# Attention outputs split on GpSimd and turned by DMA, with the K projection, its store and its stack at earlier steps

## The chip, the cores and the metric

One core of a Trainium2 chip runs the whole kernel. The metric is the device time of one execution in microseconds (us). Engines are named as in the profile: PE is TensorE's matmul, PEld its weight load, DVE is VectorE, ACT is ScalarE, POOL is GpSimd, and SP is SyncE, whose queue issues nearly all DMAs here.

## What is computed

A gated cross-attention block and a gated mixture of experts, for 16 sequences of 512 tokens, 256 wide:

```python
x = x + tanh(g_xattn) * (attention(layernorm(x), ctx) @ Wo.T + bo)    # 16 heads of 16, causal, softmax
x = x + tanh(g_ffn) * experts(layernorm(x))                           # 8 experts, each takes the top 128 tokens of a sequence
```

The mask is causal over the context too, so only the first 512 of its 1601 rows count. Float32 results come out of bf16 matmuls by splitting a number into a high part (its bf16 rounding) and a low part (what is left, in bf16), and summing three products for each 128 rows of the contraction.

## The kernel before

The program has two phases. `attention` takes the first 890 us or so, `experts` the rest; the change touches the first alone.

**Bodies and steps.** `steps(b)` (lines 77 to 122) writes the order of the attention phase out by hand. A body b has 4 groups of heads, g = 0 to 3, and 11 steps in each, k = 0 to 10. Below, *step 2.3* is g = 2, k = 3. In step g.k stands first the unit `max` of (b, g, k): matmuls of Q by K into one of three PSUM banks in turn, whose row maximum DVE takes (4 reductions over whole units of small tiles, 8 custom instructions for the 384 and 512 wide tiles); so PE can be three units ahead of DVE and no more. Behind it stands `sc` for k up to 9, the scores of the group two earlier, whose exponential ACT takes and whose diagonal blocks POOL zeroes (`affine_select`, behind `sc` 7, 8 and 9). Then come the pieces of the table `extra`. Every engine walks the same list and does its own part of each piece, in that order, so that a piece that waits holds up all pieces behind it on its engine. `rounds` (line 290) runs the bodies -1 to 17: -1 fills, 16 and 17 drain, 3 to 13 are a loop. One body works for several sequences: `max` for b, the projections for b + 1, the end of the attention for b - 1, and output, second layernorm and router for b - 2.

**The pieces that the texts speak of.**
- `ln1`, `ln1+`: statistics and application of the first layernorm (DVE, lines 628 to 641; a power on POOL, line 773). `xsplit`, `csplit`: POOL splits the layernorm's output and the context into high and low parts, a bf16 cast (line 792) and a subtraction (line 794) for each half. `xturn`, `cturn`: SP issues two DMA transposes (line 348).
- `q`, `k`, `v`: projections (PE, lines 510 and 523). `q+`, `k+` take the results to three bf16 parts (ACT line 604, DVE line 685, POOL lines 778 and 780). `qstore`, `kstore` write them to DRAM (SP, line 340), `qstack`, `kstack` load them stacked by group (SP, line 360).
- `mt`, `mt+`, `mrow`: the row maxima are turned by PE (line 485), split (ACT line 588, DVE line 671), and written by two small DMAs (line 370) into the rows that `sc` of that group contracts with. `mt` of (b, g) stands a group behind its maxima.
- `pv`, `pv+`: probabilities by V into one bank (PE line 477), copied by ACT. `yt`: PE turns the result back (line 490). `yt+`: DVE divides by the sum into `yq` (lines 693 and 697).
- `yb`: PE turns half of `yq`, 128 columns, with four float32 transposes (line 500). `yb+`: ACT takes the high part (line 599), DVE the low part (line 677), into `ynT`. `o`: PE multiplies by Wo (line 523). `o+`: DVE adds to the residual (line 709).

**Banks.** All of `yt`, `yb`, `mt`, `o`, `q`, `k`, `xt`, `ll`, `lt` and `v` are jobs. They use two PSUM banks in turn, in the order of the list, and `free_bank` makes each wait until the job two places before it has been read.

Of the kernel before, what the change touches and what calls it, by code (L numbers as in the profile page):

```python
# [79 lines left out]
def steps(body):  # L80
# [1147 lines left out]
```

## Time and profile before

| | |
|---|---|
| median of 3 runs | 1950.83 us (1948.68 to 1951.47) |
| the profiled execution | 1948.92 us |
| its span, first to last instruction | 1947.0 us |
| mean granted TensorE clock | 0.981 |
| PE, PEld busy | 1795.8 us (92%), 1063.0 us (55%) |
| DVE, ACT, POOL busy | 1133.9 us (58%), 893.9 us (46%), 868.6 us (45%) |
| DMA queue of SP | 204.13 MB, 44.9% of 16 engines' span |

Busy shares are averages over both phases. In the timeline of an engine a row may stand for several equal instructions (x4); a bracket at its end gives how long the engine was idle before it and what released it. The end of a matmul is modelled, about 0.16 us later than the next one's start, so on PE the time of a piece is read from start to start.

### The profile page before, as it was taken

Reading aid. Unit: us, or ns where it says so; the run is one execution under the profiler, and the core shown is the slowest. Engines: PE = TensorE matmul, PEld = TensorE weight load, DVE = VectorE, ACT = ScalarE, POOL = GpSimd, SP = SyncE. Lnnn points to the kernel's source line nnn. Section 1 sums busy time; section 2 is a strip of 40 time slices with the busy share of each in tenths; the row PEclk is TensorE's granted clock in tenths of the full one; section 3 lists DMA queues with packets and bytes.
Section 4 is the critical chain, followed back from the end, with each engine's and each line's share of the span. In section 5 each row is a group of like instructions: output and inputs, shape, how many; then the busy total and the mean of one; then the engine's idle time right before and its main releaser. Section 6 shows DMA issues by size and latency. Waiting matters only on the chain.

```text
span 1947.0 us, 41394 instructions
## 1 busy us (share of the span) xinstructions
PE 1795.8 (92%) x13478; PEld 1063.0 (55%) x13542; DVE 1133.9 (58%) x2809; ACT 893.9 (46%) x1716; POOL 868.6 (45%) x899
## 2 busy tenths in 40 slices
PE   3899999999999999981899999999999999999997
PEld 1455555555555555551365665656555656656565
DVE  2778888888888888756744344343424343443431
ACT  1366666656556666652334334343434343343332
POOL 4466666666666666445042423233233324232322
PEclk9899999999999999995999999999999999999999
DMA  6767666666666666527554564645546646445222
GB/s 150 167 153 166 161 161 171 166 164 161 169 162 155 170 160 165 136 68 183 141 109 89 101 118 86 120 95 90 106 75 121 123 87 103 83 81 96 49 31 25
DMA packets 377497, 239.30 MB, mean 123 GB/s; under 512 B 259479, under 2 KB 358943, under 8 KB 377375
## 3 DMA queue, kind: packets, MB, share of 16 engines
q1 hardware_dynamic: 352799, 204.13, 44.9%
q0 software_dynamic: 24576, 33.57, 11.0%
q8 instruction: 73, 1.20, 0.3%
q14 instruction: 49, 0.40, 0.1%
HBM read 118.63 MB, written 58.72 MB: 91 GB/s over the span
## 4 chain that ended last, share of the span: by engine, by line
PE 49%; DVE 2%; SPq 1%; DMA 1%; issue 1%; ACT 0%; POOL 0%; POOLq 0%; DVEq 0%
PE bank L1085 11%; PE bank L1084 11%; PE bank L1086 10%; PE bank L1102 6%; PE bank L1100 6%; PE bank L1101 6%; SPq L1011 1%; DVE h L1202 0%; DVE h L1205 0%; ACT h L1130 0%; DMA gate_raw<-in_L_ffn_w_gate 0%; DVE top_at L1152 0%; DVE work L1155 0%; POOL gate_nat L1029 0%; SPq L990 0%
## 5 line engine op out<-in xcount | busy, mean ns | idle before, releaser
L1050 POOL DMA_INDIRECT out<-y,row_now x128 | 202.0, 1578 | 604.4 <-ACT y L1137 579.7
L574 ACT ACTIVATE prob<-bank 128x512 f32<-128x512 f32 x640 | 368.8, 598 | 173.5 <-PE bank L463 88.1
L1202 DVE TENSOR_TENSOR h<-bank,silu 128x512 f32<-128x512 f32 x256 | 176.3, 689 | 396.7 <-PE bank L1086 262.0
L1130 ACT ACTIVATE h<-h 128x512 bf16<-128x512 f32 x256 | 161.2, 630 | 346.9 <-DVE h L1202 331.5
L661 DVE CUSTOM_DVE_ANT_0 masked<-bank,causal 128x384 f32<-128x384 f32 (+1 forms) x512 | 299.0, 616 | 35.8 <-PE bank L440 34.5
L440 PE MATMUL bank<-ks,qs 96*128 96x128 bf16 (+3 forms) x1024 | 278.3, 306 | 20.7 <-DMA ks<-k_parts 10.4
L1205 DVE TENSOR_TENSOR h<-h 128x512 bf16<-128x512 f32 x256 | 177.3, 693 | 179.6 <-ACT h L1130 173.3
L1101 PE MATMUL bank<-downT,h 128*128 128x256 bf16 x1024 | 279.1, 273 | 0.0
L1102 PE MATMUL bank<-downT,h 128*128 128x256 bf16 x1024 | 279.1, 273 | 0.0
L1100 PE MATMUL bank<-downT,h 128*128 128x256 bf16 x1024 | 279.1, 273 | 0.0
L1085 PE MATMUL bank<-tokT,gateT 128*128 128x512 bf16 x511 | 194.4, 380 | 35.4 <-DMA tokT<-rows 30.2
L813 POOL TENSOR_SCALAR_AFFINE_SELECT prob<-prob 128x512 f32<-128x512 f32 x256 | 159.2, 646 | 110.5 <-ACT prob L574 110.4
L460 PE MATMUL bank<-qs,ks 128*128 128x128 bf16 x1024 | 198.6, 220 | 3.2 <-ACT prob L574 0.9
L1084 PE MATMUL bank<-tokT,upT 128*128 128x512 bf16 x511 | 194.4, 380 | 6.8 <-DVE h L1202 6.7
L463 PE MATMUL bank<-qs,ks 98*128 98x384 bf16 (+2 forms) x768 | 196.3, 273 | 0.0
L1085 PE MATMUL bank<-tokT,upT 128*128 128x512 bf16 x512 | 194.6, 380 | 0.1
L1086 PE MATMUL bank<-tokT,upT 128*128 128x512 bf16 x512 | 194.6, 380 | 0.0
L477 PE MATMUL bank<-prob,v_aug 128*32 128x512 f32 (+3 forms) x2048 | 190.5, 444 | 1.4 <-ACT yT L582 1.4
L1084 PE MATMUL bank<-tokT,gateT 128*128 128x512 bf16 x481 | 182.8, 380 | 2.5 <-ACT silu L1124 0.9
L440 PEld LDWEIGHTS bank<-ks,qs 96*128 96x128 bf16 x1024 | 99.3, 98 | 154.7 <-issue 60.9
L1086 PE MATMUL bank<-tokT,gateT 128*128 128x512 bf16 x481 | 182.9, 380 | 0.1
L1137 ACT ACTIVATE y<-bank,gate_now 128x256 f32<-128x256 f32 x128 | 53.7, 470 | 260.8 <-PE bank L1102 260.8
(146 smaller groups left out, 2931.0 us busy)
## 6 DMA issues: line engine op xcount, KB each, us to landing
q_parts<-q_sb SPq DMA_DIRECT2D x64, 192.0 KB, 2.9
k_parts<-k_sb SPq DMA_DIRECT2D x64, 192.0 KB, 2.9
qs<-q_parts SPq DMA_DIRECT2D x64, 192.0 KB, 2.9
ks<-k_parts SPq DMA_DIRECT2D x64, 192.0 KB, 3.3
x_t<-in_x SPq DMA_DIRECT2D x16, 512.0 KB, 3.9
ctx_t<-in_ctx SPq DMA_DIRECT2D x16, 512.0 KB, 4.8
qs<-q_parts SPq DMA_DIRECT2D x64, 128.0 KB, 2.9
ks<-k_parts SPq DMA_DIRECT2D x64, 128.0 KB, 3.2
```

The source lines that it names most:

```text
L440: last = nc.tensor.matmul(dst[:, h * w:(h + 1) * w], qs[0:STACK, gr, h0 + h, i * P:(i + 1) * P], ks[0:STACK, gr, h0 + h, 0:w], start=True, ...
L460: last = nc.tensor.matmul(dst[:, at:at + P], ks[:, gr, h0 + h, j * P:(j + 1) * P], qs[:, gr, h0 + h, j * P:(j + 1) * P], start=True, stop= ...
L463: last = nc.tensor.matmul(dst[:, at + P:at + PWIDTH[j]], ks[0:ROWS, gr, h0 + h, j * P:(j + 1) * P], qs[0:ROWS, gr, h0 + h, (j + 1) * P:T], ...
L574: nc.scalar.activation(prob[:, gr % 2, h0:h0 + nh, POFF[tiles[0]]:POFF[tiles[0]] + w], sc_bank[SC_BANK[k]][:, 0:nh * w].rearrange("p (h w) ...
L661: nc.vector.tensor_tensor_reduce(masked[:, k % 2, 0:w], max_bank[max_at(gr, k)][:, 0:w], causal[:, T - w:T], 1.0, LOWEST, ALU.add, ALU.max ...
L1050: nc.gpsimd.indirect_dma_start(out_rows, bass.IndirectOffsetOnAxis(ap=row_now[:, par, c, s:s + 1], axis=0), y[:, c % 2, s, :], None, compu ...
L1084: nc.tensor.matmul(banks[it % 2][:, :], hi, xh, start=(dh == 0), stop=False)
L1085: nc.tensor.matmul(banks[it % 2][:, :], hi, xl, start=False, stop=False)
L1086: last = nc.tensor.matmul(banks[it % 2][:, :], lo, xh, start=False, stop=(dh == NH2 - 1))
L1100: nc.tensor.matmul(to, hh, wh, start=(it == 0), stop=False)
L1101: nc.tensor.matmul(to, hh, wl, start=False, stop=False)
L1102: last = nc.tensor.matmul(to, hl, wh, start=False, stop=(it == IT - 1))
```

## The change

- `yb` and `yb+` go. In their place stand `ysplit` on POOL (a cast and a subtraction on half of `yq`, into `y_nat`) and `yturn` on SP (one DMA transpose of that half, both parts, into `ynT`, which has another layout). `o` waits for the transposes, and `yt+` waits for `ysplit` where it waited for `yb`.
- Half 0 is split at step 1.3 and turned at step 1.6, half 1 at 3.3 and 3.9, where `yturn` stands behind the stacks.
- `ln1+` goes from steps 0.0 and 0.1 to 0.2 and 0.4, `xsplit` from 0.1 and 0.2 to 0.3 and 0.5, `xturn` from 0.5 to 0.7.
- The K projection goes from steps 2.4 and 2.5 to 2.1 and 2.4, `kstore` from 3.0 to 2.9, `kstack` of group 0 from 3.6 to 3.3.
- `mt` of group 1 goes from step 2.1 to 2.2, its `mrow` from 2.2 to 2.3. `pv` of group 3 goes from steps 2.1, 2.2, 2.4, 2.5 to 2.3, 2.5, 2.6, 2.7, its `pv+` from 2.7 to 2.9, `yt` and `yt+` of group 2 from 2.3 and 2.2 to 2.7 and 2.6, `qstack` of group 0 from 3.3 to 3.1.
- `masked`, the output of DVE's custom instruction that nothing reads, becomes bf16.

```diff
     extra = {
-        0: {0: [("pv", b - 1, 1, 0), ("ln1+", b + 1, 0)],
-            1: [("yt", b - 1, 0), ("pv", b - 1, 1, 1), ("xsplit", b + 1, 0), ("ln1+", b + 1, 1)],
-            2: [("yt+", b - 1, 0), ("yb", b - 2, 1), ("xsplit", b + 1, 1)],
+        0: {0: [("pv", b - 1, 1, 0)],
+            1: [("yt", b - 1, 0), ("pv", b - 1, 1, 1)],
+            2: [("yt+", b - 1, 0), ("ln1+", b + 1, 0)],
...
-            3: [("yt", b - 1, 2), ("yb", b - 1, 0), ("yb+", b - 1, 0), ("k+", b + 1, 0)],
...
-    masked = sb(ctx, "masked", [P, 2, T], F32)
+    masked = sb(ctx, "masked", [P, 2, T], BF16)
...
+                elif kind == "yturn":
+                    half = p[2]
+                    hold(split_lo["y"], count(b, 2, half + 1))
+
+                    hold(filled["o"], count(b, 2, 0))
+                    sp.dma_start_transpose(ynT[:, half, :, :, :].rearrange("p r i t -> p (r i) t"),
+                                           y_nat[:, half, :, :, :].rearrange("p r i d -> p (r i d)"))\
+                        .then_inc(flipped["y"], 16)
...
-                            wait(pe, read["yb"], count(b, 2, 2))
+                            wait(pe, flipped["y"], count(b, 32, 32))
...
-                elif kind == "yb+":
-
-                    half = p[2]
-                    wait(dve, hi_done[job], count(b, 2, half + 1))
-                    nc.vector.tensor_tensor(ynT[:, 1, half, :], src[:, :], ynT[:, 0, half, :], ALU.subtract)\
-                        .then_inc(read[job], 1)
...
-                    wait(dve, filled["yb"], count(b, 2, gr // 2 - 1))
+                    wait(dve, split_lo["y"], count(b, 2, gr // 2 - 1))
...
+                elif kind == "ysplit":
+                    half = p[2]
+                    wait(pool, read["yt"], count(b, GROUPS, 2 * half + 2))
+
+                    wait_apart(pool, flipped["y"], count(b, 32, 16 * half - 16), passed["pool"])
+                    src = yq[:, :, half * P:(half + 1) * P]
+                    nc.gpsimd.tensor_copy(y_nat[:, half, 0, :, :], src).then_inc(split_hi["y"], 1)
+                    wait(pool, split_hi["y"], count(b, 2, half + 1))
+                    nc.gpsimd.tensor_tensor(out=y_nat[:, half, 1, :, :], in0=src, in1=y_nat[:, half, 0, :, :],
+                                            op=ALU.subtract).then_inc(split_lo["y"], 1)
```

The places where the order of instructions moves most are shown as rows of each engine's program, in the body behind the loop (b = 14), which has the loop's order. `ISA` is the custom maximum, and the lines of the changed kernel are a few higher or lower than before.

DVE at the start of group 0, before (`mx` are the maxima of steps 0.0 to 0.3):

```order
L666 TENSOR_REDUCE mx<-bank 128x4
L641 TENSOR_SCALAR xn<-x_t,ln_mv,ln_rstd 128x256 x2
L666 TENSOR_REDUCE mx<-bank 128x2
L641 TENSOR_SCALAR xn<-x_t,ln_mv,ln_rstd 128x256 x2
L666 TENSOR_REDUCE mx<-bank 128x2
L693 RECIPROCAL rden<-bank 128x16
L697 TENSOR_TENSOR yq<-bank,rden 128x4x64
L661 ISA masked,mx<-bank,causal 128x384
L661 ISA mx 128x1
L677 TENSOR_TENSOR ynT<-bank,ynT 128x512
```

and now:

```order
L667 TENSOR_REDUCE mx<-bank 128x4
L667 TENSOR_REDUCE mx<-bank 128x2 x2
L688 RECIPROCAL rden<-bank 128x16
L692 TENSOR_TENSOR yq<-bank,rden 128x4x64
L642 TENSOR_SCALAR xn<-x_t,ln_mv,ln_rstd 128x256 x2
L662 ISA masked,mx<-bank,causal 128x384
L662 ISA mx 128x1
```

The division into `yq` now stands ahead of both halves of the layernorm, and the second half of the layernorm two steps further down.

PE at steps 2.1 and 2.2, before, from the end of the scores of step 2.1:

```order
L460 MATMUL bank<-qs,ks 128x128
L463 MATMUL bank<-qs,ks 128x256
L460 MATMUL bank<-qs,ks 128x128
L485 MATMUL bank<-ident,mx 16x128
L477 MATMUL bank<-prob,v_aug 32x512 x4
L440 MATMUL bank<-ks,qs 128x256
L444 MATMUL bank<-mask_qk,identb 128x128
L440 MATMUL bank<-ks,qs 128x256
L444 MATMUL bank<-mask_qk,identb 128x128
L460 MATMUL bank<-qs,ks 128x128
L463 MATMUL bank<-qs,ks 128x384
L477 MATMUL bank<-prob,v_aug 32x384 x4
```

and now:

```order
L469 MATMUL bank<-qs,ks 128x128
L472 MATMUL bank<-qs,ks 128x256
L469 MATMUL bank<-qs,ks 128x128
L515 MATMUL bank<-cT,wkT 128x512 x6
L449 MATMUL bank<-ks,qs 128x256
L453 MATMUL bank<-mask_qk,identb 128x128
L449 MATMUL bank<-ks,qs 128x256
L453 MATMUL bank<-mask_qk,identb 128x128
L469 MATMUL bank<-qs,ks 128x128
L472 MATMUL bank<-qs,ks 128x384
L494 MATMUL bank<-ident,mx 16x128
L449 MATMUL bank<-ks,qs 128x384
```

Six matmuls of K, and the maximum of step 2.2, now stand between the start of group 2 and the turn of the maxima of group 1, and the `pv` matmuls stand behind it.

SP at the end of group 0 and in group 1, now (before, the row with `ynT` was not there):

```order
L349 DMA_TRANSPOSE cT<-c_nat 128x8x128 x2
L146 ISA
L356 DMA_TRANSPOSE ynT<-y_nat 128x8x128
L146 ISA
L146 REGISTER_ALU
L379 DMA qs<-m_sb 1x16x128 x2
```

The transpose of `yq`'s first half stands between the context's transposes and the rows of the maxima of group 0.

## Rows read from the trace of the kernel before

**Rows 1.** Groups 0 to 3 of a body: us, busy PE, PEld, DVE, ACT, POOL, clock, DMA.

```profile
495.94:509.73 13.79, 12.42 (x123) 8.09 (x124) 12.10 (x35) 7.39 (x14) 9.57 (x12) 1.00 0.58 157
509.73:520.96 11.23, 11.01 (x99) 5.54 (x99) 10.24 (x34) 7.23 (x15) 5.40 (x8) 1.00 0.64 136
520.96:535.13 14.17, 13.26 (x115) 7.07 (x115) 11.24 (x30) 8.25 (x17) 9.71 (x11) 1.00 0.81 223
535.13:547.12 11.99, 11.85 (x131) 7.83 (x132) 9.34 (x32) 8.03 (x18) 7.69 (x10) 1.00 0.53 132
```

**Rows 2.** Timeline of PE, body at 496 to 547 us: groups 0 to 2.

```profile
500.13 0.60 PE L500 MATMUL bank<-ident,yq 128*128 128x128 f32 x4
500.56 0.33 PE L440 MATMUL bank<-ks,qs 96*128 96x384 bf16 x1
...
503.50 0.27 PE L485 MATMUL bank<-ident,mx 128*16 128x128 f32 x1 [1.31 <-DVE yq L697]
...
513.51 1.46 PE L510 MATMUL bank<-xT,wqT 128*128 128x512 bf16 x6
...
520.90 0.23 PE L440 MATMUL bank<-ks,qs 96*128 96x128 bf16 x1 [0.22 <-DVE mx L661]
...
523.10 0.28 PE L485 MATMUL bank<-ident,mx 128*16 128x128 f32 x1 [0.79 <-DVE mx L661]
...
525.76 0.34 PE L440 MATMUL bank<-ks,qs 96*128 96x384 bf16 x1
...
527.58 1.47 PE L510 MATMUL bank<-cT,wkT 128*128 128x512 bf16 x6
```

**Rows 3.** Timeline of DVE in the same body, groups 0 to 2.

```profile
499.06 0.74 DVE L641 TENSOR_SCALAR xn<-x_t,ln_mv,ln_rstd 128x256 f32<-128x256 f32 x2
...
500.31 1.74 DVE L641 TENSOR_SCALAR xn<-x_t,ln_mv,ln_rstd 128x256 f32<-128x256 f32 x2
...
503.76 0.69 DVE L677 TENSOR_TENSOR ynT<-bank,ynT 128x512 bf16<-128x512 f32 x1
...
506.29 0.75 DVE L709 SCALAR_TENSOR_TENSOR x<-bank,tanh_g,res_t 128x512 f32<-128x512 f32 x1 [0.71 <-PE bank L523]
...
510.74 1.88 DVE L666 TENSOR_REDUCE mx<-bank 128x4 f32<-128x512 f32 x3
...
524.23 1.27 DVE L666 TENSOR_REDUCE mx<-bank 128x4 f32<-128x512 f32 x2
```

**Rows 4.** Timeline of POOL in the same body.

```profile
500.05 0.61 POOL L792 CAST x_nat<-xn 128x512 bf16<-128x512 f32 x1 [1.02 <-DVE xn L641]
...
506.52 1.17 POOL L794 TENSOR_TENSOR c_nat<-ctx_t,c_nat 128x512 bf16<-128x512 f32 x1
508.24 0.65 POOL L813 TENSOR_SCALAR_AFFINE_SELECT prob<-prob 128x512 f32<-128x512 f32 x1 [0.55 <-ACT prob L574]
...
516.67 0.61 POOL L778 CAST q_sb<-rest 128x512 bf16<-128x512 f32 x1 [5.41 <-DVE rest L685]
...
544.53 1.81 POOL L813 TENSOR_SCALAR_AFFINE_SELECT prob<-prob 128x512 f32<-128x512 f32 x3 [3.52 <-ACT prob L574]
```

**Rows 5.** Timeline of the SP queue in the same body: start us, us of issue, DMA.

```profile
506.82 2.67 SPq L348 DMA_TRANSPOSE xT<-x_nat  x2
...
513.08 2.60 SPq L348 DMA_TRANSPOSE cT<-c_nat  x2
516.05 1.18 SPq L370 DMA_DIRECT2D qs<-m_sb  x2
```

**Rows 6.** Landing time of all transposes of line 348 (first), of all rows of line 370 (second).

```profile
DMA to landing us min/median/max: 3.2/3.3/5.4
...
DMA to landing us min/median/max: 1.6/1.7/3.7
```

**Rows 7.** Timeline of all engines behind the last attention output, drain.

```profile
870.84 0.63 PE L500 MATMUL bank<-ident,yq 128*128 128x128 f32 x4
...
873.12 2.78 PE L523 MATMUL bank<-woT,ynT 128*128 128x256 bf16 x24 [1.66 <-DVE ynT L677]
```

More of the change, by code:

```diff
@@ L114, in steps @@
+        3: {1: [("mt", b, 2), ("qstack", b + 1, 0)],
+            2: [("mrow", b, 2), ("mt+", b, 2), ("yt", b - 1, 3), ("yt+", b - 1, 3)], 3: [("ll+", b - 2), ("kstack", b + 1, 0), ("ysplit", b - 1, 1)],
             4: [("pv", b, 0, 0), ("ll", b - 2), ("v", b + 1, 0, 0), ("v", b + 1, 0, 1), ("v+", b + 1, 0)],
-            5: [("ln1", b + 2, 0)], 6: [("kstack", b + 1, 0), ("lt", b - 2), ("lt+", b - 2), ("pv", b, 0, 1)],
+            5: [("ln1", b + 2, 0)], 6: [("lt", b - 2), ("lt+", b - 2), ("pv", b, 0, 1)],
@@ L116, in steps @@
             8: [("v+", b + 1, 1), ("v", b + 1, 1, 0), ("pv", b, 0, 2), ("v", b + 1, 1, 1)],
-            9: [("qstack", b + 1, 1), ("kstack", b + 1, 1)], 10: [("pv+", b, 0), ("pv", b, 0, 3), ("save", b - 2), ("ln1", b + 2, 1)]},
+            9: [("qstack", b + 1, 1), ("kstack", b + 1, 1), ("yturn", b - 1, 1)], 10: [("pv+", b, 0), ("pv", b, 0, 3), ("save", b - 2), ("ln1", b + 2, 1)]},
     }
@@ L266, in attention @@
     read = {n: sem(f"{n}_read") for n in JOBS_A_BATCH}
[L267 removed]
+    hi_done = {n: sem(f"{n}_hi_done") for n in ("q", "k", "mt")}
     rest_split = sem("rest_split")
[L269 to L271 removed]
+    split_hi = {n: sem(f"{n}_hi_split") for n in ("x", "c", "y")}
+    split_lo = {n: sem(f"{n}_lo_split") for n in ("x", "c", "y")}
+    flipped = {n: sem(f"{n}_flipped") for n in ("x", "c", "y")}
     max_filled, max_read = sem("max_filled"), sem("max_read")
@@ L491, in piece @@
                     last.then_inc(filled[kind], 1)
-                elif kind in ("yb", "xt"):
+                elif kind == "xt":
                     half = p[2]
-                    src = {"yb": yq, "xt": xn2}[kind]
-                    if kind == "yb":
-                        wait(pe, read["yt"], count(b, GROUPS, 2 * half + 2))
-                    else:
-                        wait(pe, ln_done["ln2"], count(b, NT, NT))
+                    wait(pe, ln_done["ln2"], count(b, NT, NT))
                     for i in range(NT):
-                        last = nc.tensor.transpose(to[:, i * P:(i + 1) * P], src[:, i, half * P:(half + 1) * P],
+                        last = nc.tensor.transpose(to[:, i * P:(i + 1) * P], xn2[:, i, half * P:(half + 1) * P],
                                                    ident[:, :])
@@ L589, in piece @@
                         .then_inc(hi_done["mt"], 1)
-                elif kind in ("yb+", "xt+"):
+                elif kind == "xt+":
                     half = p[2]
-                    dst, user, per = {"yb": (ynT, "o", 2), "xt": (xn2T, "ll", 1)}[job]
-                    wait(act, filled[job], count(b, 2, half + 1))
-                    wait(act, filled[user], count(b, per, 0))
-                    if job == "xt":
-                        nc.scalar.activation(dst[:, half, :], src[:, :], ACT.Copy).then_inc(read[job], 1)
-                    else:
-                        nc.scalar.activation(dst[:, 0, half, :], src[:, :], ACT.Copy).then_inc(hi_done[job], 1)
+                    wait(act, filled["xt"], count(b, 2, half + 1))
+                    wait(act, filled["ll"], count(b, 1, 0))
+                    nc.scalar.activation(xn2T[:, half, :], src[:, :], ACT.Copy).then_inc(read["xt"], 1)
                 elif kind in ("q+", "k+"):
```

38 lines of the change are left out of this document (17 added, 21 removed).

## The prediction, made before the changed kernel was run

> **What bounds the kernel now.** I first split a body of the attention phase into its four groups. The stretches of [rows 1] begin at the first mask matmul of each group and end at that of the next body: 13.79 + 11.23 + 14.17 + 11.99 = 51.18 us. PE is busy for 12.42 + 11.01 + 13.26 + 11.85 = 48.5 of them, DVE for 42.9, POOL for 32.4, at a granted clock of 1.00. So PE is the main bound, DVE lies close behind, and PE is idle above all in groups 0 and 2. The timeline of PE [rows 2] then says which waits these are. Reading starts of rows: the turn of the maxima at step 0.4 starts at 503.50 after 1.31 us idle, released by the division into `yq`, since its bank was held by the earlier `yt`. The turn at step 2.1 starts at 523.10 after 0.79 us idle, released by DVE's last maximum of group 1, and the first `max` of group 2 at 520.90 waited 0.22 us, for DVE too. Matmul ends are modelled late, so each true stall is about 0.15 us longer than shown: 1.45 + 0.95 + 0.4 = 2.8 us of a body.
>
> The timeline of DVE [rows 3] shows why. From the start of the body to the maxima of group 2 at 524.23 it has one gap of 0.71 us (it waits for the first `o`). Inside stand the second half of `ln1+`, 1.74 us from 500.31 on, ahead of the division, and `yb+`'s subtraction at 503.76. DVE enters group 1 at 510.74, when PE entered it at 509.7, and enters group 2 at 524.23, when PE was there at 520.90: it is 3.3 us behind. **So in groups 0 and 1 DVE paces the body, in groups 2 and 3 PE does.** What counts is what each side loses in its own part, and where the one hands over to the other.
>
> **The change, part by part.**
>
> *PE, `yb` goes.* Four transposes take from 500.13 to the next start at 500.56 [rows 2], 0.43 us, and there are two sets in a body. The set in group 2 lies where PE paces: -0.44. The one in group 0 lies where DVE paces: 0 by itself, since it is covered by DVE's run.
>
> *DVE, `yb+` goes.* The row at 503.76 has 0.69 us, of which 0.08 overlap the next start (the maxima at 510.74 show 1.88 for three, so about 0.6 each): -0.61 in group 0, where DVE paces. The one in group 2 is covered by DVE's gaps there. ACT's copy of 0.6 us is in ACT's idle time; nothing waits for it afterwards.
>
> *DVE, `ln1+` behind the division.* `yq` is now ready after three reductions, and the turn at step 0.4 does not wait: PE gets 1.31 us earlier to `o`, and with that the 0.71 us gap on DVE before `o+` goes. In return the maximum of step 0.2 is now reached by DVE before PE has made it: PE makes it just before its `yb` at 500.13, DVE would be there at about 499.4. I charge 0.5 us for it, less 0.2 for the wait for the layernorm's power, which vanishes as there is now time for it. Sum of the two edits on DVE's run: -0.61 - 0.71 + 0.5 - 0.2 = about **-1.0 us** in a body. Bounds: 0 (all of it comes back as waits for PE and `o`) and -1.5.
>
> *Hand-over in group 2.* The stall of 0.95 us at the turn is filled by K's six matmuls of 1.47 us (527.58, [rows 2]). PE now runs until `max` of step 2.3, which needs the reading of step 2.0. In the trace that ends at 524.23 + 0.6 = 524.83, and PE stands at step 2.3 at 525.76: 0.93 us can be won between them. The second half of K at step 2.4 needs DVE's `rest` of the first, some 2 us behind the reading of 2.0, and takes back 0.2: **-0.7 us**. Bounds: 0 and -0.95. What is queued behind: `pv` of group 3 with its copy, now two steps later, and `yt`, which DVE's division waits for at step 2.6. From PE's `yt` to the turn at 3.1 there are some 4 us of PE's work by the places of the same pieces in the trace (an estimate), and DVE needs 0.5 + 0.65 + 4 x 0.61 = 3.6 for the division and four maxima: no wait, by 0.4.
>
> *POOL, `ysplit`.* A cast of 0.61 and a subtraction of 1.17 us [rows 4], twice: 3.6 us a body. The first is covered by the 5.41 us that POOL waits for `rest` before 516.67, the second by the 3.52 us before 544.53. Without that cover the q parts or the zeroing of `prob` would be up to 1.8 us late. Tighter is what moves with `ln1+`: the four splits ran from 500.05 to 507.7, ahead of the first zeroing at 508.24. Now the second split of x can begin only at about 505.0, so the zeroing begins at 505.0 + 1.85 + 3.6 = 510.4 and its first block is there at 511.0. `pv` of step 1.3 stood at 512.10, and stands at 511.1 now: 0, with no margin.
>
> *SP, `yturn`.* A pair of transposes is issued in 2.67 us [rows 5], so one holds the queue for 1.3 us; it lands 3.3 us after its issue, 5.4 at worst [rows 6]. `o` needs half 1 some 6 us after its issue at 3.9: covered. Half 0 stands ahead of `mrow` of group 0, and with x's transposes at 506.9 the chain is 509.6, stacks to 512.5, context's transposes to 515.3, `yturn` (POOL is done at 514.8) to 516.9, second row of `mrow` at 517.8, landed after 1.7 us [rows 6] at 519.5. `sc` of step 2.0 needs it 0.5 us behind the `max` at 520.90, that is 520.3 now: covered by 0.8. x's transposes land at 511.6, for `q` at 513.51 - 1.0. `kstack` of group 0 gets more time, not less. DMA share is 0.53 to 0.81 in [rows 1]: it holds two more transposes.
>
> *`masked` in bf16.* The custom instruction reads PSUM and takes 0.61 us from start to start; nothing reads its output. 0, bounds -0.1 and +0.1 us each, with no row for it.
>
> *Drain.* Behind the last division `yb` starts at 870.84 and `o` at 873.12 [rows 7]: 2.3 us. Now 1.8 (POOL) + 0.1 + 3.3 (landing) + 0.1 = 5.3, from about 870.4: **+2.6 us, once**. The last body also wins `yb` and a part of the turn's stall, -1.
>
> *Sum.* -0.44 - 1.0 - 0.7 = -2.1 us in a body of 51.18, in 14 bodies (1 to 14), -29.4; body 0 has neither `yb` nor `o` and stays; drain and last body +1.6. The profiled execution of 1948.92 would become 1921.1, and the median stands 1.9 above it: **1923 us**.
>
> **A rule weighed against the rows.** The second pair of `ln1+` took 1.74 us where a pair takes 0.74 when POOL is idle, and POOL's split began at 500.05, just before it [rows 3, 4]. The Trainium skill, SBUF — State Buffer, section Who interferes with whom, says that DVE in a two-port mode and GpSimd exclude each other for a whole instruction, whoever starts first. By that rule, the trace agrees. By the rule alone 3.6 us more on POOL would be up to 3.6 us more of blocked DVE in a body; by the rows, the two `ysplit` lie at about 512.6 to 514.8 and 541 to 543, where DVE has no `xn` to write.
>
> **The rivals.**
> 1. *The gain is halved by what becomes tight in group 1.* POOL's chain of splits, or x's transposes, come 0.5 to 1.5 us late for `pv` at 1.3 or `q` at 1.4. For: no margin above. Against: the second `ln1+` can come earlier than I reckoned. Gain 1.0 a body: 1950.8 - 14 + 1.6 = 1938.
> 2. *Slower: `mrow` behind `yturn`.* If a transpose takes its 5.4 us or `mrow` its 3.7 [rows 6], `sc` at step 2.0 stalls PE. The margin is 0.8, and the gain up to there is 2.1, so it decides from 2.9 us behind my chain on. At 4 us, it costs 1.1 net: 1950.8 + 15.4 + 1.6 = 1968. Against: the same small DMAs land in 1.7 at the median, and in the trace they stand right behind the context's transposes already (516.05, [rows 5]).
> 3. *DVE blocked by the new splits* (as POOL's split did to the pair of `xn` at 500.31). If each `ysplit` blocks DVE for one instruction of 1.17, 2.3 us a body take the gain away: 1950.8 + 0.2 x 14 + 1.6 = 1955, at the edge of what can be told. Against: the position of the `xn` rows.
> 4. *More gain:* all 2.8 us of stalls and `yb` in both groups go, because DVE catches up faster: 3.5 a body, 1950.8 - 49 + 1.6 = 1903.
>
> **How the numbers follow.** Forecast (1.6 to 2.8 us a body, 1913 to 1930) 0.50; rival 1 0.22; rival 4 0.12; rival 2 0.10; rival 3 0.06. The range takes in rivals 1 and 4 up to the point at which 2 in 10 are left: 1903 to 1944. A measurement tells 0.2%, 3.9 us, from no change. Faster: 0.50 + 0.22 + 0.12 = 0.84; within: 0.04 from rival 3 and the edge of 2; slower 0.12.
>
> **What would show it.** In the changed profile: no idle time at the turn of the maxima at 0.4 and 2.1; the DVE idle time before `o+` gone; PE busy down by some 0.9 us a body; the body at 49.1 us; POOL up by 3.6 us a body; `o` of the last sequence 5 us behind its division. Wrong would be: PE idle before `pv` released by POOL's zeroing (rival 1), PE idle before `sc` of a group released by the DMA of `m_sb` (rival 2), or `xn` rows over 1.3 us in more places (rival 3).

## The result, and the profile after

| | before | changed |
|---|---|---|
| median, in the same job | 1949.36 us (1948.45 to 1951.47, 5 runs) | 1928.59 us (1926.94 to 1929.9, 5 runs) |
| ratio to before, 95% interval | | 0.9891 [0.9879, 0.9902] |
| profiled execution, span | 1948.92, 1947.0 us | 1929.9, 1928.1 us |

The change gains 1.1%. The prediction said 1923.0 us, 1903 to 1944, with 0.84 on faster; the time is 5.6 us above the predicted one, inside the range.

The first section of the page and its row of SP's queue, changed kernel. PE has 14.5 us less than before, DVE 21.3 less, POOL 53.8 more, and the queue moves 8.4 MB more:

```profile
PE 1781.3 (92%) x13350; PEld 1052.6 (55%) x13414; DVE 1112.6 (58%) x2777; ACT 871.7 (45%) x1684; POOL 922.4 (48%) x963
...
q1 hardware_dynamic: 386591, 212.53, 47.6%
```

The four groups of the body at 485 to 534 us, with the columns of [rows 1]:

```profile
485.40:497.80 12.40, 11.97 (x118) 7.57 (x119) 11.10 (x34) 6.62 (x13) 6.69 (x8) 1.00 0.63 172
497.80:509.33 11.53, 11.09 (x99) 5.56 (x100) 10.24 (x34) 7.19 (x14) 9.88 (x14) 1.00 0.92 180
509.33:522.35 13.02, 12.35 (x111) 6.87 (x112) 10.88 (x29) 7.41 (x15) 11.10 (x13) 1.00 0.81 225
522.35:534.40 12.05, 11.91 (x133) 7.77 (x132) 9.22 (x32) 8.20 (x19) 8.00 (x10) 1.00 0.55 150
```

The body is 49.00 us long where it was 51.18: -1.39 in group 0, +0.30 in group 1, -1.15 in group 2, +0.06 in group 3, together -2.18. The nine bodies 4 to 12 repeat 49.00 within 0.02.

The timeline of PE in that body. The turn of the last maxima (491.04) and that of step 2.2 (512.38) have no idle time any more; four shorter waits are left. Read from start to start they are 0.60 us at step 1.0, 0.38 before `pv` at 1.3, 0.40 at 2.0 and 0.84 at 2.3:

```profile
491.04 0.27 PE L494 MATMUL bank<-ident,mx 128*16 128x128 f32 x1
...
497.73 0.23 PE L449 MATMUL bank<-ks,qs 96*128 96x128 bf16 x1 [0.43 <-DVE mx L662]
...
500.46 1.07 PE L486 MATMUL bank<-prob,v_aug 128*32 128x512 f32 x8 [0.22 <-POOL prob L818]
...
509.26 0.23 PE L449 MATMUL bank<-ks,qs 96*128 96x128 bf16 x1 [0.22 <-DVE mx L662]
...
512.38 0.27 PE L494 MATMUL bank<-ident,mx 128*16 128x128 f32 x1
513.32 0.34 PE L449 MATMUL bank<-ks,qs 96*128 96x384 bf16 x1 [0.67 <-DVE mx L667]
```

The timeline of DVE, answering to [rows 3]. The gap before `o+` (494.58) is gone, and a gap of 0.59 us before the maximum of step 0.2 has come. That maximum is the third and last reduction of its group; eight custom instructions follow it (the text ahead of the prediction counts four reductions):

```profile
489.56 0.69 DVE L667 TENSOR_REDUCE mx<-bank 128x2 f32<-128x512 f32 x1 [0.59 <-PE bank L453]
...
490.55 0.42 DVE L692 TENSOR_TENSOR yq<-bank,rden 128x256 f32<-128x256 f32 x1
490.89 0.72 DVE L642 TENSOR_SCALAR xn<-x_t,ln_mv,ln_rstd 128x256 f32<-128x256 f32 x2
...
492.69 1.50 DVE L642 TENSOR_SCALAR xn<-x_t,ln_mv,ln_rstd 128x256 f32<-128x256 f32 x2
...
494.58 0.74 DVE L704 SCALAR_TENSOR_TENSOR x<-bank,tanh_g,res_t 128x512 f32<-128x512 f32 x1
...
498.82 1.88 DVE L667 TENSOR_REDUCE mx<-bank 128x4 f32<-128x512 f32 x3
```

The timeline of POOL. From 494.38 on it has no idle time up to the split of `yq` that follows the zeroing, where [rows 4] show it idle before the first zeroing:

```profile
491.87 0.61 POOL L787 CAST x_nat<-xn 128x512 bf16<-128x512 f32 x1 [3.39 <-DVE xn L642]
...
494.38 0.61 POOL L787 CAST x_nat<-xn 128x512 bf16<-128x512 f32 x1 [0.66 <-DVE xn L642]
...
499.77 2.41 POOL L818 TENSOR_SCALAR_AFFINE_SELECT prob<-prob 128x512 f32<-128x512 f32 x4
502.13 0.61 POOL L797 CAST y_nat<-yq 128x512 bf16<-128x512 f32 x1
502.82 1.16 POOL L799 TENSOR_TENSOR y_nat<-yq,y_nat 128x512 bf16<-128x512 f32 x1
```

The queue of SP with the new transpose between the context's and the rows of the maxima, as in [rows 5]:

```profile
502.64 2.63 SPq L349 DMA_TRANSPOSE cT<-c_nat  x2
505.54 1.23 SPq L356 DMA_TRANSPOSE ynT<-y_nat  x1
507.13 1.17 SPq L379 DMA_DIRECT2D qs<-m_sb  x2
```

The landing time of all 32 transposes of line 356:

```profile
DMA to landing us min/median/max: 3.1/3.3/4.9
```

**Where the span went.** It fell by 18.9 us. The ten bodies 4 to 13 give -21.8, bodies 2 and 3 -3.9. Bodies 1 and 14 give nothing (+0.2, -0.2), body 0 takes 3.9 and what lies before it 0.2, and what comes behind the start of body 15 takes 2.7. In body 14 of this execution PE waited 1.30 us for a row of the maxima, behind that wait the granted clock was 0.50 in the window shown below, and the body was 50.84 us. The timeline of PE at the wait, and the window behind it with the columns of [rows 1]:

```profile
755.70 0.23 PE L469 MATMUL bank<-qs,ks 128*128 128x128 bf16 x1 [1.30 <-DMA qs<-m_sb]
...
756.00:759.40 3.40, 3.40 (x14) 1.63 (x13) 2.27 (x4) 1.20 (x2) 3.10 (x4) 0.50 0.88 221
```

In the two runs below with next to the same order (`masked` in float32, `mrow` first) that body was 48.3 and 48.7 us, so the size of the loss changes from one execution to another.

### The profile page after: what moved, and what is told of

Its sections match the earlier page's. It is cut to its first block, busy times and chain, and to the rows that moved or that the text cites. A ratio compares the mean times of both kernels' runs of the same rounds, so it can differ in the third digit from the quotient of the medians.

```text
span 1928.1 us, 41223 instructions
## 1 busy us (share of the span) xinstructions
PE 1781.3 (92%) x13350; PEld 1052.6 (55%) x13414; DVE 1112.6 (58%) x2777; ACT 871.7 (45%) x1684; POOL 922.4 (48%) x963
## 3 DMA queue, kind: packets, MB, share of 16 engines
q1 hardware_dynamic: 386591, 212.53, 47.6%
## 4 chain that ended last, share of the span: by engine, by line
PE 49%; DVE 2%; SPq 1%; DMA 1%; issue 1%; POOL 1%; ACT 0%; POOLq 0%
PE bank L1090 11%; PE bank L1089 11%; PE bank L1091 10%; PE bank L1107 6%; PE bank L1106 6%; PE bank L1105 6%; SPq L1016 1%; DMA gate_raw<-in_L_ffn_w_gate 1%; DVE h L1207 0%; DVE h L1210 0%; ACT h L1135 0%; SPq L995 0%; DVE top_at L1157 0%; POOL gate_nat L1034 0%; POOL up_nat L1034 0%
## 5 line engine op out<-in xcount | busy, mean ns | idle before, releaser
L662 DVE CUSTOM_DVE_ANT_0 masked<-bank,causal 128x384 bf16<-128x384 f32 (+1 forms) x512 | 300.4, 616 | 51.5 <-PE bank L449 49.5
L1042 POOL DMA_INDIRECT rows<-tokens,row_now x128 | 130.4, 1019 | 94.7 <-DVE row_now L1198 56.9
```

What stands on the lines that cost most here:

```text
L662: nc.vector.tensor_tensor_reduce(masked[:, k % 2, 0:w], max_bank[max_at(gr, k)][:, 0:w], causal[:, T - w:T], 1.0, LOWEST, ALU.add, ALU.max ...
```

## The experiments

One theory was the prediction's: the turn at step 0.4 is freed because `ln1+` goes behind the division. The rival that the first comparison suggested: it is freed because `yb` leaves the list of jobs, so that the turn gets the other PSUM bank. Times are medians with their ranges; a body's length is read from mask matmul to mask matmul in the middle of the loop of the profiled run, where it repeats. The diffs show only part of each edit.

### The path of y alone, and the moves alone

The first of these keeps the whole old order and has only `ysplit` and `yturn` for `yb` and `yb+`. The second is the kernel before, with `yb` and `yb+`, and every other piece moved as in the change (`yb` of half 0 at step 2.6, half 1 as it was).

```diff
 # order of before, y alone
-            2: [("yt+", b - 1, 0), ("yb", b - 2, 1), ("xsplit", b + 1, 1)],
+            2: [("yt+", b - 1, 0), ("xsplit", b + 1, 1)],
...
 # kernel before, moves alone
-            2: [("yt+", b - 1, 0), ("yb", b - 2, 1), ("xsplit", b + 1, 1)],
+            2: [("yt+", b - 1, 0), ("yb", b - 2, 1), ("ln1+", b + 1, 0)],
```

> The schedule of before, with yb and yb+ taken out and ysplit and yturn put at the changed kernel's steps: the new path of the attention output alone. My theory: 0.44 us of PE in group 2 and 0.61 us of DVE in group 0, so the body takes 50.1 to 50.5 us instead of 51.18, body 0 stays at 39.0, the drain loses 3.7 us; the whole 1939 to 1943 us. Rival, that the new work on POOL and SP costs something in the loop which the moves hide: body 50.8 or more, the whole 1947 or more.

> The kernel before, with PE's yb and its two copies kept (half 1 at steps 0.2 and 0.3, half 0 at 2.6), but every other piece at the changed kernel's step: the moves alone. My theory: they are worth 1.1 us of the 2.18 us a body, so 50.0 to 50.3 us, body 0 takes 42.9 us (3.9 lost), no loss in the drain; the whole 1937 to 1941 us. Rival, that the moves only mend what the new path of y would cost: body 51.0 or more and the whole above 1950 us.

Measured: y alone (with `masked` in bf16 too) 1931.23 us (1929.03 to 1933.17), ratio 0.9899 [0.9882, 0.9915], body 49.57; moves alone 1935.74 (1930.94 to 1938.38), ratio 0.9918 [0.9897, 0.9939], body 49.46. The groups of the body:

| us | g0 | g1 | g2 | g3 | body |
|---|---|---|---|---|---|
| before | 13.79 | 11.23 | 14.17 | 11.99 | 51.18 |
| y alone | 12.76 | 11.24 | 13.58 | 11.99 | 49.57 |
| moves alone | 12.58 | 11.35 | 13.48 | 12.05 | 49.46 |
| changed | 12.40 | 11.53 | 13.02 | 12.05 | 49.00 |

The parts gain 1.61 and 1.72 alone and 2.18 together, so they overlap by 1.15, most of it (0.85) in group 0: -1.03 and -1.21 alone, -1.39 together. In group 2 they nearly add up (-0.59 and -0.69 make -1.28, measured -1.15). Both rivals fall (bodies of 50.8 and 51.0 or more), but both theories were too cautious as well: 50.1 to 50.5 and 50.0 to 50.3 were expected, and the totals are below the ranges given. In the whole time the path of y alone gains about as much as the full change (ratios 0.9899 and 0.9891, with intervals that overlap), since it doesn't lose in body 0. PE in the run with y alone: the turn at 0.4 doesn't wait, and PE waits one step later, for the maxima; the turn at 2.1 waits as it did before:

```profile
491.34 0.34 PE L449 MATMUL bank<-ks,qs 96*128 96x384 bf16 x1 [0.84 <-DVE mx L667]
...
510.72 0.28 PE L494 MATMUL bank<-ident,mx 128*16 128x128 f32 x1 [0.78 <-DVE mx L662]
```

With the moves alone the turn doesn't wait either, since the division is early (it starts at 493.16, 5.15 us into the body that began at 488.01, where the kernel before had it at 7.00), and what is left in group 0 is a short wait of the first `o` for `yb+`:

```profile
495.45 1.47 PE L523 MATMUL bank<-woT,ynT 128*128 128x256 bf16 x12 [0.34 <-DVE ynT L677]
```

### One move taken back at a time

The changed kernel, with `ln1+`, `xsplit` and `xturn` at their old steps; and the changed kernel with groups 2 and 3 in the old order.

```diff
 # x back
-            4: [("mt+", b - 1, 3), ("mt", b - 1, 3), ("ln1+", b + 1, 1)],
+            4: [("mt+", b - 1, 3), ("mt", b - 1, 3)],
...
 # K back
-            4: [("k", b + 1, 1, 0), ("k", b + 1, 1, 1)],
+            4: [("k", b + 1, 0, 0), ("k", b + 1, 0, 1), ("pv", b - 1, 3, 2)],
```

> The changed kernel with ln1+, xsplit and xturn back at the steps they had before (0.0 and 0.1, 0.1 and 0.2, 0.5). The changed kernel's loop body takes 49.00 us and its body 0 takes 42.9 (51.18 and 39.0 before). My theory, that the division into yq ahead of the layernorm frees PE and DVE in group 0: the idle time before the turn of the maxima at step 0.4 comes back (over 1 us), the body takes 49.8 to 50.3 us, and body 0 returns to 39.0 to 39.5, since its loss comes from the late x transposes. In all 14 x 1.0 - 3.8, 1936 to 1942 us. Rival, that the gain is the removed work of yb alone and the places of ln1+ do not matter: the body stays within 0.3 us of 49.0 and the whole, with body 0 mended, comes to 1925.

> The changed kernel with all of groups 2 and 3 in the order of before (K projection at 2.4 and 2.5, mt at 2.1, kstore at 3.0, kstack at 3.6, pv and yt of that group as before), only ysplit and yturn kept. My theory, that K fills the hand-over from DVE to PE in group 2: the idle time of about 0.8 us at the turn of step 2.1 is back, the body takes 49.6 to 49.9 us, the whole 1937 to 1941 us. Rival, that PE waits for the same reading of DVE in any order: the body within 0.2 us of 49.0, the whole within 3 us of 1928.6.

Measured: x back 1926.94 us (1925.02 to 1930.45), ratio 0.9877 [0.986, 0.9893], body 49.07, groups 0 and 1 at 12.76 and 11.24, exactly those of y alone. K back 1930.65 (1930.09 to 1931.75), ratio 0.9892 [0.9876, 0.9909], body 49.50, group 2 at 13.57. So beside the new path of y the move of `ln1+` is worth 0.07 us: it wins 0.36 in group 0 and gives 0.29 back in group 1, where its splits keep POOL busy up to the zeroing. The theory of the first run (49.8 to 50.3) falls, its rival holds. Body 0 did not return to 39.0 to 39.5 there: it took 41.34, with a granted clock of 0.87 in its group 2.

Groups 2 and 3 in their new order are worth 0.50 a body in the loop. That lies between the theory (49.6 to 49.9) and the rival (within 0.2 of 49.0). In the whole time neither move shows: the ratios of both runs are within 0.2% of the changed kernel's 0.9891, with intervals that overlap it, since the changed order loses in body 0 and at the loop's ends about what it wins in the loop. The total of K back, 1930.65, is in the rival's range.

### Which bank, which order

Two runs change the bank of the turn at step 0.4 without the rest. In the first, y has its new path in the old order, and the turn is put into the bank of `yt` of group 0, as it was before. In the second, the kernel before has the turn and its split at step 0.1, ahead of `yt`.

```diff
 # bank held
+JOB_BANK.update({("mt", 3): JOB_BANK["yt", 0], ("o", 0): 1 - JOB_BANK["yt", 0], ("o", 1): JOB_BANK["yt", 0]})
...
 # turn first, kernel before
-            1: [("yt", b - 1, 0), ("pv", b - 1, 1, 1), ("xsplit", b + 1, 0), ("ln1+", b + 1, 1)],
+            1: [("mt+", b - 1, 3), ("mt", b - 1, 3), ("yt", b - 1, 0), ("pv", b - 1, 1, 1), ("xsplit", b + 1, 0), ("ln1+", b + 1, 1)],
...
-            4: [("mt+", b - 1, 3), ("mt", b - 1, 3)],
```

> The new path of y alone (as in e3, whose body takes 49.57 us), with three PSUM banks of jobs exchanged so that the turn of the maxima at step 0.4 uses the bank of yt of step 0.1 and so waits for the division into yq, as it did before the change, where yb stood between them. New theory: the wait at step 0.4 went because taking yb out of the list of jobs gave the turn the other bank, and not because of ln1+. Then the idle time of about 1.3 us before that turn is back, released by DVE's division, and the body takes 50.3 to 50.9 us. Rival, that DVE paces group 0 anyway: the idle time is back but the body stays within 0.3 us of 49.57, since DVE is at the same place.

> The kernel before, with only the turn of the last maxima and its split (mt, mt+) moved from step 0.4 to step 0.1, ahead of yt, so that the bank which it takes isn't the division's. Theory (the bank order, not the order on DVE, made the 1.31 us wait at step 0.4): the wait goes, body 49.9 to 50.4 us instead of 51.2, total 1934 to 1940. Rival (the wait only moves to yt or yb, which now want the bank that mt+ reads): body 50.9 to 51.4, total 1946 to 1953.

Bank held: 1950.68 us (one run), bodies of 52.0 and 50.5 in turn, 51.24 on average. The wait is back, 1.74 us in each body: the 1.31 of before and the 0.43 that PE then spent on `yb`. Two bodies in a row, PE:

```profile
453.49 0.38 PE L495 MATMUL bank<-ident,mx 128*16 128x128 f32 x1 [1.74 <-DVE yq L693]
...
455.13 2.33 PE L529 MATMUL bank<-woT,ynT 128*128 128x256 bf16 x12
...
505.49 0.27 PE L495 MATMUL bank<-ident,mx 128*16 128x128 f32 x1 [1.74 <-DVE yq L693]
```

The windows behind the wait in the two bodies, with the columns of [rows 1]:

```profile
453.40:455.50 2.10, 2.02 (x14) 0.94 (x15) 1.71 (x7) 0.86 (x2) 2.02 (x3) 0.52 0.36 120
505.40:507.50 2.10, 2.01 (x22) 1.45 (x23) 1.61 (x7) 0.86 (x2) 2.02 (x3) 1.00 0.37 124
```

So the mean of 51.24 holds two costs. In the bodies whose granted clock stays at 1.00, the body is 50.49 us and group 0 is 13.67, where y alone had 12.76 and the kernel before 13.78: the wait itself takes back all but 0.11 us of what y's path gained in group 0, and the gain in group 2 (13.59, 14.17 before) stays. That body is inside the theory's 50.3 to 50.9; the rival's 49.57 falls. The other bodies are 1.5 us longer, and behind the same wait their granted clock fell (0.52 in the window shown). The edit also puts `yt` of group 1 behind the second `o` in one bank; PE doesn't wait there.

The timeline of DVE, with the division that PE waits for:

```profile
504.93 0.42 DVE L693 TENSOR_TENSOR yq<-bank,rden 128x256 f32<-128x256 f32 x1
```

Turn first: 1949.67 us (1946.97 to 1957.8, 10 runs), ratio 1.0007 [0.9994, 1.002], body 51.12. My theory expected 49.9 to 50.4 and falls; the rival's 50.9 to 51.4 holds. The turn itself doesn't wait (499.22). PE waits in two places behind it instead, for the split of the turned maxima before `yb`, and for `yb+` before `o`. The first of the two, 0.32 us, the edit brought itself, since `yb` now has the bank of the turn:

```profile
499.22 0.27 PE L484 MATMUL bank<-ident,mx 128*16 128x128 f32 x1
...
501.69 0.65 PE L499 MATMUL bank<-ident,yq 128*128 128x128 f32 x4 [0.32 <-DVE m_sb L670]
...
505.50 0.72 PE L522 MATMUL bank<-woT,ynT 128*128 128x256 bf16 x5 [0.88 <-DVE ynT L676]
```

Taken together: in the old order PE wanted two results that DVE made behind `ln1+`: the division, through the bank, and `yb+`, through `o`. With only the one or only the other removed (these two runs), group 0 is 13.67 and 13.73 us where it was 13.78: next to nothing is gained there. y's path removes both at once, and the moves make both early.

### Two parts that were put at nothing

```diff
 # masked in float32 again
-    masked = sb(ctx, "masked", [P, 2, T], BF16)
+    masked = sb(ctx, "masked", [P, 2, T], F32)
...
 # mrow ahead of yturn, step 1.8
-            6: [("yturn", b - 1, 0), ("q", b + 1, 1, 0), ("q", b + 1, 1, 1), ("q+", b + 1, 1)],
-            7: [("pv", b - 1, 2, 2)], 8: [("mrow", b, 0)],
+            6: [("q", b + 1, 1, 0), ("q", b + 1, 1, 1), ("q+", b + 1, 1)],
+            7: [("pv", b - 1, 2, 2)], 8: [("mrow", b, 0), ("yturn", b - 1, 0)],
```

> The changed kernel with masked in float32 again and nothing else. Theory that the output type of DVE's custom instruction does not count: body 49.0 us as in the changed kernel, the custom instruction 685 and 548 ns as before. Rival, that bf16 makes it cheaper: a body longer by 0.3 us or more and a longer instruction.

> The changed kernel with yturn of half 0 at step 1.8 behind mrow of group 0, instead of 1.6 ahead of it. In the changed kernel PE waits 1.47 us in body 14, and less in body 1, for the rows of the maxima behind that transpose, and nowhere in the loop. Theory: the loop body stays at 49.00 us, body 14 falls from 50.8 to 49.3 us, the whole comes down by 1 to 2 us, to 1927. Rival, that the queue limits the loop too: a body of 48.7 us or less and the whole under 1924.

`masked` in float32: 1924.9 us (one run), body 49.00; the 512 custom instructions take 300.3 us, 300.4 in the changed kernel. `mrow` first: 1927.67 us (1926.72 to 1928.86), ratio 0.9893 [0.9876, 0.9909], body 49.00. Neither matters in the loop. At the loop's two ends the place of `mrow` does: in the changed kernel PE waits for the rows of the maxima before `sc` of step 2.0 by 0.86 us in body 3 and 1.30 in body 14, with `masked` in float32, the same order, by 0.78 and 0.29, and with `mrow` first in no body. Body 14 took 48.70 us there, where 49.3 was expected.

### Can the rest be won?

Four runs on the waits that the changed kernel still has. `ln2+` (the second layernorm's application, DVE) stands at 1.9 and 1.10, where DVE is behind; `xs` (its split on POOL) with it. The first run moves `ln2+` to 2.3 and 2.4 and `xs` to 2.5, the third has `xs` at 3.4. The second puts the first half of `ln1+` at 0.1, into DVE's gap, and POOL's splits one step or more earlier. The fourth has the second's and the third's edits, and the old table for body 0 alone.

```diff
 # ln2 later (xs at 2.5) / ln2 and xs (xs at 3.4)
-            9: [("pv", b - 1, 2, 3), ("xs", b - 2), ("ln2+", b - 2, 1)],
-            10: [("pv+", b - 1, 2), ("ln2+", b - 2, 0)]},
+            9: [("pv", b - 1, 2, 3)],
+            10: [("pv+", b - 1, 2)]},
...
 # x fill
+            1: [("yt", b - 1, 0), ("pv", b - 1, 1, 1), ("ln1+", b + 1, 0)],
+            2: [("yt+", b - 1, 0), ("xsplit", b + 1, 0), ("csplit", b + 1, 0)],
...
 # combined, with the table of before for body 0
+    if isinstance(b, int) and b == 0:
+        extra = {
```

> The changed kernel with the application of the second layernorm (two pairs of DVE instructions, 2.4 us) moved from steps 1.9 and 1.10 to 2.3 and 2.4, and its split on POOL from 1.9 to 2.5. Theory that DVE paces groups 0 and 1 and the hand-over in group 2: PE's stalls of 0.40 us at step 2.0 and 0.84 us at step 2.3 go, the body takes 47.6 to 48.2 us, the whole 1911 to 1918 us. Rival, that the work only moves the wait to a later step: the body 48.7 us or more and PE idle in group 2 for DVE at a later step, or for the transposes of xn.

> The changed kernel, with the first pair of ln1+ at step 0.1 (where DVE idles 0.59 us before the custom maximum of step 0.2), the splits of x and of the context one step or more earlier on POOL, the second pair at 0.4 as it is. Theory (what is left of DVE's lag and POOL's chain in group 0 still sets the stalls of 0.60 us at step 1.0 and 0.38 us before pv at 1.3): both shrink, body 48.2 to 48.7 us instead of 49.0, total 1918 to 1925. Rival (these stalls are set by the readings of the banks before, not by the layernorm's place): body 49.0, total 1927 to 1930.

> The changed kernel, with ln2+ at steps 2.3 and 2.4 instead of 1.9 and 1.10, and xs on POOL at 3.4. Theory (DVE's lag at the end of group 1 makes the 0.84 us stall in group 2, and the run with xs at 2.5 lost it again because xs delayed POOL's zeroing): the stall in group 2 goes and none comes before pv of step 3.4; body 47.8 to 48.4 us, total 1913 to 1921. Rival (the lag only moves to group 3, since DVE's work is the same and group 3 has no slack for it): body 49.0 to 49.3, total 1927 to 1932.

> Both edits of the two runs before, and body 0 alone in the order of the old table with the new path of y. Theory (body 0 lost its 3.9 us only through its order, where PE is idle anyway, and the edits add up): body 0 at 39.1 us, the later bodies 47.3 to 48.0, total 1903 to 1914. Rival (the old order of body 0 only passes its debt on to body 1, and the two edits do not add up): body 1 longer by 2 us or more, later bodies 48.3 or more, total 1918 to 1926.

| | median us (range) | ratio [95%] | g0 | g1 | g2 | g3 | body |
|---|---|---|---|---|---|---|---|
| ln2 later | 1931.88 (1930.92 to 1933.48) | 0.9917 [0.9901, 0.9934] | 12.41 | 11.51 | 12.38 | 12.96 | 49.25 |
| x fill | 1921.56 (1918.31 to 1923.05) | 0.9859 [0.9844, 0.9874] | 12.00 | 11.23 | 13.03 | 12.05 | 48.32 |
| ln2 and xs | 1922.91 (1919.96 to 1924.07) | 0.9862 [0.9847, 0.9877] | 12.40 | 11.54 | 12.38 | 12.08 | 48.40 |
| combined | 1916.17 (1912.46 to 1919.93) | 0.9832 [0.9817, 0.9847] | 12.00 | 11.24 | 12.46 | 12.26 | 47.96 |

*ln2 later* takes the 0.64 us out of group 2 and puts 0.91 into group 3; the theory of 47.6 to 48.2 us falls. POOL, in that run, is at `xs` (lines 823 and 825) when the first diagonal block wants its zeroing. The zeroing (526.11) and, behind it, the copy of V that the first `pv` also needs (line 810) come late, and `pv` at 3.4 starts when that copy is done (the profile names no releaser here; the link is read from the times and the program). Three rows of POOL and, last, that of PE:

```profile
524.02 2.13 POOL L825 TENSOR_TENSOR tok<-xn,tok 128x1024 bf16<-128x1024 f32 x1
526.11 0.64 POOL L818 TENSOR_SCALAR_AFFINE_SELECT prob<-prob 128x512 f32<-128x512 f32 x1
526.69 1.04 POOL L810 COPY v_aug<-v_new 128x1024 f32<-128x1024 f32 x1
...
527.83 1.06 PE L486 MATMUL bank<-prob,v_aug 128*32 128x512 f32 x8 [0.83 <-issue]
```

*ln2 and xs* differs from it only in the place of `xs` and keeps the gain: group 3 is back at 12.08 (12.05 to 12.42 from body to body; this run and *combined* do not repeat exactly). That shows `xs` to be the cause of the miss before. Its body is at the upper edge of the 47.8 to 48.4 expected, and its total is above the 1913 to 1921: in that execution body 0 took 45.32 us and body 3 50.02. *x fill*, whose theory holds in body and total, removes the wait before `pv` at 1.3 and halves that at 1.0 (0.31 from start to start): -0.40 in group 0 and -0.30 in group 1. *combined* is the best version: 32.8 us below the kernel before (1948.93 in that job), and by the two ratios (0.9832 against 0.9891, with intervals that don't meet) 0.6% or 11.5 us below the changed one. Its body falls to 47.96 where I hoped for 47.3 to 48.0. Its groups:

```profile
481.11:493.11 12.00, 11.85 (x118) 7.56 (x119) 11.20 (x34) 6.42 (x13) 8.39 (x10) 1.00 0.67 178
493.11:504.35 11.24, 11.02 (x98) 5.56 (x99) 10.25 (x34) 7.18 (x14) 8.21 (x12) 1.00 0.93 185
504.35:516.81 12.46, 12.34 (x110) 6.90 (x111) 11.03 (x29) 7.28 (x15) 7.28 (x11) 1.00 0.78 212
516.81:529.07 12.26, 11.92 (x133) 7.78 (x132) 9.77 (x32) 8.41 (x19) 11.73 (x13) 1.00 0.57 171
```

The total, 1916, is outside the 1903 to 1914 expected. Body 0 came out at 40.61 us and not at 39.1, and body 3 at 50.58: PE waits there for a row of the maxima (1.26 us), and group 2 has a granted clock of 0.89. Giving it the old order did not give it the old banks: these are handed out once, from the order of the loop, and by it both halves of K fall into one bank there. PE waits 1.03 us for the first half's remainder (group 2 of body 0, line 548); the rest of that group's 12.15 us, 9.35 with y alone, goes with a granted clock of 0.86 in place of 1.00:

```profile
79.67 1.47 PE L548 MATMUL bank<-cT,wkT 128*128 128x512 bf16 x6 [1.03 <-DVE rest L713]
```

## Why the prediction was right, and where it was wrong

**The size of the loop's gain: right.** 2.1 us a body was forecast, 2.18 measured. The turns at 0.4 and, in its new place, 2.2 have no idle time, PE's busy time fell by 0.9 us a body (14.5 in 16), and POOL's rose by 3.4. *Group 2:* -0.44 for `yb` and -0.7 for the hand-over, -1.14; measured -1.15. The moves alone show the hand-over by itself at -0.69; taken out of the changed kernel it is worth 0.50. The path of y alone gives 0.59 in this group, so that the sum fits to 0.01 is in part luck. What takes its place is the wait of 0.84 at `max` 2.3, which I had only as "0.93 us can be won between them". *Groups 0 and 1:* -1.0 forecast, -1.09 measured (-1.39 and +0.30). The gap of 0.5 us on DVE before step 0.2 came (0.59), and the gap before `o+` went. The reading that DVE has one gap from the start of the body to 524.23 was wrong: it has two more, 0.39 us before the first maximum (498.22), for PE, and 0.78 before `rest` (515.81), for ACT.

**The step that failed: "DVE, `ln1+` behind the division".** I gave the turn's freedom, and with it the 0.71 us gap, to the move of `ln1+`. With `ln1+` put back the body is 49.07 against 49.00. The mechanism is real, since the moves alone free the turn with `yb` still there, but it was not needed: taking `yb` out of the list of jobs shifts every job behind it, up to the place of the second `yb`, to the other bank, so the turn no longer follows `yt` in its bank. I had the sentence on the banks and did not count the list through. The sum was right because both ways remove the same wait once, and that is luck: the four terms of DVE's run (-0.61, -0.71, +0.5, -0.2) do not describe what freed the turn, since y's path gives -1.03 in group 0 with `ln1+` where it was. Had I priced the two edits apart, by what each gives alone, it would have been 1.15 too high.

**Rival 1 held in part.** PE is idle before `pv` released by POOL's zeroing, the mark I had named for it, with 0.38 us of stall, and the 0.60 at step 1.0 belongs to the same late DVE. That is the +0.30 of group 1. I had written "0, with no margin"; it cost 0.3, not the 0.5 to 1.5 of the rival, and the gain was not halved.

**Rival 2 did not come in the steady loop, and came at its two ends.** In the body shown `mrow` is issued at 507.13 and the `sc` that needs it doesn't wait, and with `mrow` ahead of `yturn` the body is the same to 0.01 us. But its mark, PE idle before `sc` released by the DMA of `m_sb`, stands in body 3 (0.86 us) and in body 14 (1.30 us, and the slow clock behind it); it stands nowhere in the attention phase of the kernel before, and nowhere with `mrow` first.

**Rival 3 did not come.** Beside the split of `yq` at 502.13 to 503.98, DVE's rows keep their durations (a custom maximum 0.53 us). The pair of `xn` at 492.69 took 1.50 us beside POOL's subtraction from 492.56 on, where the pair at 490.89 took 0.72; the body has no more pairs over 1.3 us than before. The Trainium skill, SBUF — State Buffer, section Who interferes with whom, has the two engines exclude each other for a whole instruction where DVE is in a two-port mode. By that rule, the trace agrees.

**Body 0: "stays" was wrong, by 3.9 us.** I had looked for `yb` and `o`, found neither there, and stopped. But the moved pieces are in body 0 too, and there PE has nothing to cover them. PE in the changed kernel, body 0:

```profile
65.49 2.72 PE L515 MATMUL bank<-xT,wqT 128*128 128x512 bf16 x6 [1.23 <-DMA xT<-x_nat]
...
78.77 1.47 PE L515 MATMUL bank<-cT,wkT 128*128 128x512 bf16 x6 [0.94 <-DVE rest L680]
```

The x transposes are issued at 60.74 instead of 58.98, and `q` waits for them; K's second half waits for `rest` of the first. Group 2 of body 0 is 10.84 or 10.85 us in each run with K moved and the clock at 1.00, 9.35 or 9.36 with K in its old place: +1.5. Group 1 is 12.34 where it was 9.99: +2.35, with the clock at 0.65 in place of 0.73. With the order of the change the whole body 0 is 42.3 to 44.2 us long in one execution and another (42.28 with `masked` in float32, 44.22 with `mrow` first). With y alone, body 0 is 39.07 as before.

**The filling bodies.** "14 bodies" counted bodies 1 to 3 in full; body 1 gained nothing, bodies 2 and 3 gained 2.3 and 1.6.

**The drain: right in size, with a part missing.** From the division to `o` it was 3.15 us (869.97 to the `o` of [rows 7]), and is 852.36 - 846.76 = 5.60 now: +2.45 for +2.6 forecast. The division before the change, on DVE:

```profile
869.97 0.42 DVE L697 TENSOR_TENSOR yq<-bank,rden 128x256 f32<-128x256 f32 x1
```

The timeline of POOL in the drain, changed kernel, with the split of `yq`:

```profile
847.25 0.61 POOL L797 CAST y_nat<-yq 128x512 bf16<-128x512 f32 x1 [0.43 <-DVE yq L692]
847.94 1.15 POOL L799 TENSOR_TENSOR y_nat<-yq,y_nat 128x512 bf16<-128x512 f32 x1
```

The queue of SP behind it, with the transpose:

```profile
849.12 1.24 SPq L356 DMA_TRANSPOSE ynT<-y_nat  x1
```

PE, at `o`:

```profile
852.36 4.05 PE L528 MATMUL bank<-woT,ynT 128*128 128x256 bf16 x24 [4.57 <-DMA ynT<-y_nat]
```

And the windows up to `o` and over it, with the columns of [rows 1]:

```profile
846.80:852.30 5.50, 0.50 (x9) 0.14 (x1) 1.32 (x6) 0.51 (x2) 1.77 (x3) 0.62 0.38 92
852.30:856.50 4.20, 4.05 (x24) 2.94 (x24) 0.81 (x2) 0.00 (x0) 0.00 (x0) 0.68 0.56 191
```

The part that I had not counted is the last row: the 24 matmuls of `o` take 4.05 us where they took 2.78 [rows 7]. Behind the idle time the granted clock is 0.68, between the levels of 1.2 and 2.4 GHz, where it was 1.00. That is 1.3 us more, once.

**The sum again.** Against my 27.8 us of span, 18.9 came. The 8.9 between them: body 0 and its start 4.1, body 1 2.3, bodies 2 and 3 0.3, body 14 1.9, drain and end 1.1, less 0.8 that the loop gave beyond the forecast. All of the losses lie outside the bodies 4 to 13; the total was inside the range because the range was wide enough for it, not because these terms were foreseen.

**Still open.** How much of group 1 of body 0 is the late transposes and how much the clock was not separated. That the waits for the last `o` could be spared by keeping `yb` for the last bodies was not tried.

## What to carry to other kernels

When a piece is taken out of a list by which buffers are handed out in turn, write the list down before and after and see who now follows whom in each buffer; that shift can be the whole gain, or cost it. Two edits that remove the same wait are priced once, and a wait with two causes pays next to nothing until both are gone (0.05 and 0.11 us here), so each wait needs all its causes named before it is priced. Price the first and last rounds of a pipeline by themselves: a piece moved under cover in the loop stands bare in the fill and in the drain. Before a longer body is put down to a wait, look at its granted clock.

## What the runs showed of the hardware

- After 4.57 us of idle PE the same 24 matmuls took 4.05 us and not 2.78, at a granted clock of 0.68. This wait is paid twice, as time and as slower matmuls behind it.
- The same wait of 1.74 us in each body of the run with the bank held was followed by a fall of the granted clock in every second body (52.0 us; 0.52 at 453.40 to 455.50) and by 1.00 in the others (50.5 us). The first 12 matmuls of `o` took 2.17 us from start to start in the one, 1.32 in the other.
- One DMA transpose of 128 x 8 x 128 lands 3.1 to 4.9 us after its issue (median 3.3) and holds SP's queue for 1.27 at the median. The small rows of the maxima land 1.8 us after their issue at the median, 1.7 before; PE waits for them in none of the bodies 4 to 13, but by 0.86 and 1.30 us in bodies 3 and 14, and nowhere in the run in which they stand ahead of the new transpose. The Trainium skill, VectorE: DVE Perf Modes, section The three transpose paths, gives 1309 ns for one block of 128x128 by DMA; the runs here have eight blocks in a transpose and can't show one alone.
- The width of an output that nothing reads does not matter for the custom maximum: 512 of them take 300.3 us with float32, 300.4 with bf16.
